# Attention and gated FFN on one core: both heads' probabilities turned together in two 64-row tiles, values before keys

## What is computed

```python
def xattn(q, kv, Wq, Wk, Wv, Wo, bo, mask):    # 16 heads of 64
    qh, kh, vh = split_heads(q @ Wq), split_heads(kv @ Wk), split_heads(kv @ Wv)
    dots = einsum('bhid,bhjd->bhij', qh, kh) * 64 ** -0.5
    dots = where(mask or above the diagonal, -max, dots)
    attn = softmax(dots)
    return einsum('bhij,bhjd->bhid', attn, vh) -> (b, n, 1024) @ Wo + bo

x = x + tanh(g_xattn) * xattn(layernorm(x), ctx, ...)
x = x + tanh(g_ffn) * ffn(layernorm(x), ...)   # three products, absolute maxima over all of x between them
```

## Time and profile before

| what | value |
|---|---|
| median of 3 runs | 1734.68 us (1733.4 to 1737.57) |
| the profiled execution's own time | 1733.58 us |
| its span, first to last instruction | 1731.8 us |
| PE / DVE / ACT / POOL busy | 96% / 77% / 67% / 28% of the span |
| mean granted TensorE clock | 0.982 |
| attention, some | 1150 us of it |

### The profile page before, as it was taken

The page is one execution under the profiler, slowest core; times in us unless marked ns, Lnnn a source line. Parts: engine busy times, 40 slices in busy tenths (PEclk is TensorE's granted clock), DMA queues, the critical chain, the costliest instruction groups (busy, mean ns, idle before and its releaser), DMA issues. The chain is left out here.

```text
span 1731.8 us, 40384 instructions
## 1 busy us (share of the span) xinstructions
PE 1657.9 (96%) x14196; PEld 1407.6 (81%) x14196; DVE 1334.1 (77%) x2273; ACT 1162.8 (67%) x3061; POOL 493.5 (28%) x367
## 2 busy tenths in 40 slices
PE   8999999999999999999999999989997998986998
PEld 6788888888888888888888888878885876875998
DVE  7867768677777786776867778867887999898785
ACT  5656666666566665666666656657676999895665
POOL 2332323223223233232332322310002765560000
PEclk9999999999999999999999999989998999997999
DMA  4110001001100011010100110026775885664664
GB/s 142 67 40 27 28 22 50 24 26 36 30 34 24 26 36 38 26 36 14 50 24 26 36 38 13 14 86 239 283 276 188 298 289 209 230 248 168 212 212 144
DMA packets 60002, 173.55 MB, mean 100 GB/s; under 512 B 4528, under 2 KB 34352, under 8 KB 57008
## 3 DMA queue, kind: packets, MB, share of 16 engines
q1 hardware_dynamic: 59952, 172.90, 28.9%
HBM read 96.86 MB, written 76.02 MB: 100 GB/s over the span
## 5 line engine op out<-in xcount | busy, mean ns | idle before, releaser
L386 POOL TENSOR_TENSOR prob<-prob,rsums 128x512 f32<-128x512 f32 x254 | 266.7, 1050 | 783.5 <-DVE rsums L582 640.7
L428 ACT ACTIVATE prob<-masked,neg_max 128x128 f32<-128x128 f32 x1024 | 396.4, 391 | 77.5 <-DVE neg_max L560 76.5
L428 ACT ACTIVATION_READ_ACCUMULATOR prob<-masked,neg_max 128x1 f32 x1024 | 194.3, 190 | 0.0
L560 DVE TENSOR_REDUCE neg_max<-masked 128x4 f32<-128x512 f32 x254 | 174.3, 686 | 8.8
L558 DVE TENSOR_TENSOR masked<-score,mask_add 128x512 f32<-128x512 f32 x254 | 172.8, 680 | 0.8
L578 DVE COPY probT<-trans 128x512 f32<-128x512 f32 x126 | 86.9, 690 | 108.7 <-PE trans L792 105.8
L792 PE MATMUL trans<-ident,prob 128*128 128x128 f32 x1024 | 160.3, 279 | 0.9 <-POOL prob L406 0.8
L443 ACT ACTIVATE qT<-proj 128x512 f32<-128x512 f32 x128 | 76.7, 599 | 110.8 <-PE proj L757 110.8
L840 PE MATMUL y<-wo_hi,o_hi 128*128 128x256 f32 x508 | 145.5, 286 | 2.1 <-DVE wo_lo L508 2.0
L813 PEld LDWEIGHTS pv<-probT,v_sb 128*64 128x64 f32 x2048 | 109.7, 136 | 46.4 <-issue 44.3
L813 PE MATMUL pv<-probT,v_sb 128*64 128x128 f32 x2048 | 140.1, 279 | 6.5 <-issue 5.8
(11 more groups left out here) (251 smaller groups left out, 4588.1 us busy)
## 6 DMA issues: line engine op xcount, KB each, us to landing
gate<-gate_d SPq DMA_DIRECT2D x30, 768.0 KB, 4.5
n_x<-n_x_d SPq DMA_DIRECT2D x25, 512.0 KB, 5.0
gate_d<-stage SPq DMA_DIRECT2D x8, 1536.0 KB, 6.1
n_u_d<-w_raw SPq DMA_DIRECT2D x16, 768.0 KB, 4.0
stage<-n_u_d SPq DMA_DIRECT2D x16, 768.0 KB, 6.3
gate_d<-gate SPq DMA_DIRECT2D x7, 1536.0 KB, 6.1
x_in<-in_x SPq DMA_DIRECT2D x16, 512.0 KB, 3.9
ctx_in<-in_ctx SPq DMA_DIRECT2D x16, 512.0 KB, 3.6
```

The source lines that it names most:

```text
L386: gp.tensor_tensor(pr, pr, rsums[:, h, :].rearrange("p (b o) -> p b o", o=1).broadcast_to([P, NB, P]), ALU.mult).then_inc(normed, 1)
L428: nc.scalar.activation(prob[:, c % 2, h, b, :], masked[:, h, b, :], ACT.Exp, bias=neg_max[:, h, b:b + 1], accum_out=psums[:, h, b:b + 1]). ...
L560: nc.vector.tensor_reduce(neg_max[:, h, :], masked[:, h], X, ALU.max, negate=True).then_inc(max_done, 1)
```

## The change

Both heads' probabilities of a unit are turned together at the step's start, in 16 transposes instead of 8. Each takes 64 of the 128 queries (one half of the array's rows) and writes 64 columns: queries 0 to 63 to the bank `trans`, queries 64 to 127 to a bank of `proj`, for which `jobs` has a new job "turn" (36 jobs in a group instead of 28; `turn_bank` and `turn_job` give its bank and count). ACT copies both banks to `probT` (`copy_turned`), each copy half of every head's columns; DVE's copy goes. In PE's list the values stand before the keys, and one value job moves from step 0 to step 6. Step 6's output product stands where it does in the other steps. In step 7 t2 and t3 follow the keys directly. ACT takes both heads' exponentials before it copies `kT`; DVE takes the second reciprocal before its other work. `times_v` waits for the two copies, and in steps 0 and 4 also for that step's value copy. At attention's end the FFN's weights go through three banks instead of four.

```diff
     YC = 3
+    V_JOBS = [(0,), (1, 2), (3,), (4,), (5,), (6,), (7,), ()]
     jobs = []
     for c in range(NC):
-        jobs += [(c, "q", 0)]
+        jobs += [(c, "turn", 0), (c, "q", 0)]
         if c == NC - 1:
             jobs += [(c, "t", n) for n in range(KC)]
-        jobs += [(c, "k", 0)]
-        if c < 2:
-            jobs += [(c, "v", 2 * c), (c, "v", 2 * c + 1)]
-        elif c < 6:
-            jobs += [(c, "v", NB + c - 2)]
+        jobs += [(c, "v", n) for n in V_JOBS[c]] + [(c, "k", 0)]
     jobs += [(NC - 1, "t", n) for n in range(KC, 2 * KC)]
...
-                wait(act, transposed, 2 * (u - 2) + h + 1)
+                wait(act, transposed, u - 1)
...
+            def copy_turned(u, b, before):
+                act.wait_ge(transposed, u + 1)
+                wait(act, pv_done, u)
+                nc.scalar.activation(probT[:, :, :, 0:HALF], halves(hand.banks[0]), ACT.Copy).then_inc(first_copied, 1)
+                act.wait_ge(projected[b], before + 1)
+                nc.scalar.activation(probT[:, :, :, HALF:P], halves(proj[b]), ACT.Copy).then_inc(copied[b], 1)
             def step(g, c):
                 u, new, soft, old, more = parts(g, c)
                 if old:
-                    act.wait_ge(transposed, 2 * (u - 2) + 1)
-                    wait(act, pv_done, u - 2)
-                    nc.scalar.activation(probT[:, 0], trans[:], ACT.Copy).then_inc(probT_copied[0], 1)
+                    copy_turned(u - 2, *turn_bank(g, c, u))
...
                     exps(u - 1, c + 1, 0)
+                    exps(u - 1, c + 1, 1)
                 if new:
                     (i, _), = jobs_of(c, "k")
                     b, before = nth(g, i)
...
                 if nxt:
                     high(g, *ts[KC])
-                if soft:
-                    exps(u - 1, c + 1, 1)
-                if nxt:
                     high(g, *ts[KC + 1])
...
-                if old:
-                    dve.wait_ge(transposed, 2 * (u - 2) + 2)
-                    wait(dve, pv_done, u - 2)
-                    nc.vector.tensor_copy(probT[:, 1], trans[:]).then_inc(probT_copied[1], 1)
...
-            def transpose_prob(u, c, h):
-                pe.wait_ge(normed, 2 * u + h + 1)
-                wait(pe, probT_copied[1 - h], u + h)
-                for b in range(NB):
-                    last = nc.tensor.transpose(trans[:, b, :], prob[:, c % 2, h, b, :], ident[:])
-                last.then_inc(transposed, 1)
+            def transpose_prob(u, c, b, before):
+                pe.wait_ge(normed, 2 * u + 2)
+                wait(pe, first_copied, u)
+                wait(pe, copied[b], before)
+                pe.nop(nofuse=True)
+                to = [halves(a) for a in (hand.banks[0], proj[b])]
+                for e in range(NB):
+                    for h in range(2):
+                        for r in range(2):
+                            rows = slice(r * HALF, (r + 1) * HALF)
+                            last = nc.tensor.transpose(to[r][:, h, e, :], prob[rows, c % 2, h, e, :], ident[rows, rows])
+                            if e == NB - 1 and h == 1:
+                                last.then_inc(projected[b] if r else transposed, 1)
...
-            def times_v(u, c, then=None):
-                for h in range(2):
-                    pe.wait_ge(probT_copied[h], u + 1)
+            def times_v(u, c, b, before, then=None):
+                pe.wait_ge(first_copied, u + 1)
+                counts = {b: before + 1}
+                if c % 4 == 0 and then is not None:
+                    for i, n in jobs_of(then[1], "v"):
+                        bank, earlier = nth(then[0], i)
+                        counts[bank] = earlier + 1
+                for bank, n in counts.items():
+                    pe.wait_ge(copied[bank], n)
...
                 if old:
-                    transpose_prob(u - 2, co, 0)
+                    transpose_prob(u - 2, co, *turn_bank(g, c, u))
                 if new:
                     weights_left(g, c, jobs_of(c, "q")[0][0], 0)
...
-                if oldest and c != NC - 2:
+                if oldest:
...
-                if first or second:
-                    pe.wait_ge(w_ready, 2 if first else 5)
-                if new:
-                    weights_left(g, c, jobs_of(c, "k")[0][0], 1)
-                if old:
-                    transpose_prob(u - 2, co, 1)
-                if nxt:
-                    transpose_in(g, *ts[2])
-                if oldest and c == NC - 2:
-                    out_product(u - 3, (c - 3) % NC)
-                if first or third:
-                    pe.wait_ge(w_ready, 3 if first else 6)
+                if first:
+                    pe.wait_ge(w_ready, 3)
                 if new:
                     for i, n in jobs_of(c, "v"):
                         value(g, i, n)
+                if second:
+                    pe.wait_ge(w_ready, 5)
+                if new:
+                    weights_left(g, c, jobs_of(c, "k")[0][0], 1)
                 if nxt:
+                    transpose_in(g, *ts[2])
                     transpose_in(g, *ts[3])
                 if old:
-                    times_v(u - 2, co, (g, c, u) if new else None)
+                    times_v(u - 2, co, *turn_bank(g, c, u), (g, c, u) if new else None)
                 if new:
```

More of the change, by code:

```diff
@@ L111, in jobs_of, with turn_job @@
         return [(i, n) for i, (cc, k, n) in enumerate(jobs) if cc == c and k == kind]
+    no_turn = [jobs.index((c, "turn", 0)) for c in range(2)]
+    no_input = [i for i, (_, kind, _) in enumerate(jobs) if kind == "t"]
     def nth(g, i):
-        skipped = KC // 2 if isinstance(g, int) and g == G - 1 and i == last_k else 0
-        return i % 2, (FIRST + i) // 2 + (NJ // 2) * g - skipped
+        left_out = [a for a in no_turn if not isinstance(g, int) or g > 0 or g == 0 and a < i]
+        if isinstance(g, int) and g >= G - 1:
+            left_out += [a for a in no_input if g == G or a < i]
+        return i % 2, (FIRST + i) // 2 + (NJ // 2) * g - sum(a % 2 == i % 2 for a in left_out)
+    def turn_job(u):
+        if not isinstance(u, int):
+            return None
+        if u >= U:
+            b, before = nth(G, 0)
+            return b, before + u - U
+        return nth(u // NC, jobs_of(u % NC, "turn")[0][0])
     with ExitStack() as st:
@@ L200, in attention @@
         transposed = sem("transposed")
-        probT_copied = [sem(f"probT_copied{h}") for h in range(2)]
+        first_copied = sem("first_copied")
         pv_done = sem("pv_done")
@@ L251, in ffn_weights @@
             kind, k, h = ffn_jobs[n]
-            bank = ffn_banks[n % 4]
+            bank = ffn_banks[n % 3]
             if kind == "gate":
@@ L276, in w_part, with turn_bank @@
             return a[n][:].rearrange("p (k n) -> p k n", k=KC if n < 3 else 1)[:, :, lo:hi]
+        def turn_bank(g, c, u):
+            return turn_job(u) if isinstance(u, int) else nth(g, jobs_of(c, "turn")[0][0])
         def staged(i):
@@ L495, in _ @@
             nc.scalar.activation(o_hi[:], pv[:], ACT.Copy).then_inc(out_high, 1)
-            first_probT(U - 1)
-            for n in range(4):
+            copy_turned(U - 1, *turn_job(U + 1))
+            for n in range(3):
                 ffn_high_part(n)
@@ L500, in _ @@
             nc.scalar.activation(last_hi, hand.banks[1][:], ACT.Copy).then_inc(out_high, 1)
-            for n in range(4, len(ffn_jobs)):
+            for n in range(3, len(ffn_jobs)):
                 ffn_high_part(n)
@@ L588, in step @@
                         nc.vector.tensor_copy(v_sb[:, n % NB, cols], proj[b][:]).then_inc(copied[b], 1)
+                if soft:
+                    dve.wait_ge(exp_done, NB * (2 * (u - 1) + 2))
+                    wait(dve, normed, 2 * (u - 1))
+                    nc.vector.reciprocal(rsums[:, 1, :], psums[:, 1, :]).then_inc(recip_done, 1)
                 if nxt:
@@ L596, in step @@
                     residual(g)
-                if soft:
-                    dve.wait_ge(exp_done, NB * (2 * (u - 1) + 2))
-                    wait(dve, normed, 2 * (u - 1))
-                    nc.vector.reciprocal(rsums[:, 1, :], psums[:, 1, :]).then_inc(recip_done, 1)
                 if nxt:
@@ L726, in _ @@
             nc.vector.tensor_tensor(o_lo[:], hand.banks[1][:], o_hi[:].bitcast(F32), ALU.subtract).then_inc(out_split, 1)
-            ffn_low_part(0)
-            second_probT(U - 1)
-            for n in range(1, 4):
+            for n in range(3):
                 ffn_low_part(n)
@@ L850, in step @@
                 second = isinstance(g, int) and g == 0 and c == 1
-                third = isinstance(g, int) and g == 0 and c == 2
                 oldest = not isinstance(g, int) or 3 <= u < U + 3
@@ L933, in _ @@
                 last.then_inc(hand.x_transposed, 1)
-            for n in range(4, len(ffn_jobs)):
+            for n in range(3, len(ffn_jobs)):
                 ffn_transpose(n)
             for n in range(7 * NB):
```

(2 more changed lines are left out.)

40 lines of the change are left out of this document (15 added, 25 removed).

## The result

The changed kernel takes 1818.06 us (median of 4 runs, 1816.47 to 1821.34), the kernel before 1734.48 beside it: a ratio of 1.0481 [1.0461, 1.0502], 4.8% slower. The forecast was 1767 with a range up to 1803: the direction was right, the loss more than twice what was forecast (83 us for 33).

What follows compares the result with a forecast made beforehand. TensorE was taken to bound the kernel, busy for 1657.9 of 1731.8 us. Groups 1 to 14 add +27 us, the first about +2, the last about +4: +33 on 1734.68, said as 1767 us; range 1748 to 1803.

Steps and rivals of the forecast that it cites:

- Turning: Paired 64-row transposes at each step's start, with tile change and bare load: 0.71 us against 0.94, saving 0.23 per step.
- Rival 1: The two 64-row tiles take turns, so turning takes 0.94 and a step loses 0.21: 1816 us; chance 0.12.
- The late quarter: In six ordinary steps pv's last quarter waits for the key copy and streams 0.09 us late, bounds 0 and 0.2.
- The net of an ordinary step: Turning's saving and the late quarter in an ordinary step: -0.23 + 0.09 = -0.14 us.
- Step 4: Key copy behind eight late exponentials delays pv's last quarter: step of 9.62 us against 8.56, +1.06.
- Step 7: Fourth input transpose waits for the key copy until 8.79 us, then 2.50 to the next step: 11.29 against 9.55, +1.74.
- Added waits: Waits for normalised probabilities at a step's start covered by at least 0.5 us; step 4's value copy wait costs nothing.
- The first group: Group 0: no second statistics, but weight work on VectorE makes ScalarE wait 4.8 us for maxima; about +2 us.
- The last group's +4: No inputs to turn, but maxima waits push exponentials, five steps by 0.7 to 1.1 less 0.14; about +4 us.
- The sum: Middle group +1.95 us, groups 1 to 14 +27, with first and last group together +33 us.
- The Trainium skill's rule of the load by columns: A weight load takes columns / 1.2 ns whatever its rows; a transpose pair would last 0.11 us, turning saving nothing.

Runs made afterwards that it cites:

- Experiment 4: Changed kernel with each head turned in four full-array transposes and copied whole, instead of 64-row tiles copied in halves: 1845.86 us, 1.0656 of the kernel before.
- Experiment 2: Changed kernel with TensorE's wait for the key copy put last, behind the waits for masked scores: 1795.27 us, 1.0363 of the kernel before.
- Experiment 3: Changed kernel with twenty discarded identity transposes between step 7's third and fourth input transposes: 1802.96 us, 1.0406 of the kernel before.
- 1: Changed kernel with the key copy between the two heads' exponentials in step 7 alone: 1785.72 us, 1.0308 of the kernel before.
- 6: Changed kernel with keys in front of the values again in steps 0, 1, 3, 4 and 5: 1824.11 us, 1.0512 of the kernel before.
- 8: Kernel 7 with both layernorms' statistics in front of `o_lo` and step 7's maximum behind the first reciprocal: 1785.33 us, 1.029 of the kernel before.
- 7: Changed kernel with keys first as in 6, key wait last, and step 7's key copy between the heads' exponentials: 1775.97 us, 1.0243 of the kernel before.
- 9: Kernel 7 with step 1 as v1, k, v2, second reciprocal before value copies following keys, step 3's statistics between maxima and first reciprocal: 1733.95 us, 0.998.

## Why the prediction was right and wrong

- **Turning: right.** 0.71 us forecast; the query product starts at 0.64 and its first matmul, with its bare load of 0.11, streams at 0.75. The saving is 0.41 + 0.44 - 0.64 = 0.21, forecast 0.23. Experiment 4 has it as 0.20 to 0.24. Rival 1 (tiles take turns) is refuted by the pairs at 636.90, though its 1816 us is the time that came: a matching sum of a wrong cause.
- **The late quarter: this step failed.** "The waiting quarter then loads at 0.845 and streams at 0.90: 0.09 late", bounds 0 and 0.2. It is 0.38 late, in six steps of every group. I took a restart of 0.045 us from a step 7 row where nothing stands between the wait and the matmul; here register work and another wait stand between. Experiment 2 takes two thirds of the excess away by the order of the waits alone. The order printed ahead shows these instructions, and the prediction named them, but its upper bound didn't price them. The net of an ordinary step is +0.14 to +0.17 instead of -0.14: 6 x 0.29 = 1.7 us a group, 23 us in 13 groups.
- **Step 4: right.** 9.52, forecast 9.62; the masked scores start at 2.86 instead of 3.27, so VectorE's chain did move a little, and the slower restart gave most of that back. (The quarter streamed at 7.4 before, not at the 7.05 that the prediction says, which is step 7's number; its sum does not use it.)
- **Step 7: half.** The stall is right (8.85, forecast 8.79). **"From it to the next step 2.50: 11.29" failed**: 3.99, since the clock fell behind a wait of 1.9 us that had one of 0.3 us shortly before it. No rival had it; the cost of the clock was put at nothing. Where the clock stayed high step 7 takes 11.6, 0.3 more than forecast (PE stands 0.2 us ahead of the next turn); where it fell, 1.2 to 1.5 more than that, in ten of 13 groups. Experiment 3 gives 0.75% for all of the clock.
- **Added waits: right in the middle groups, with a mistake.** PE waits for no normalised probabilities there. Behind the last unit it does, 2.3 us where it was 0.8, which the prediction left out. And the wait of `times_v` for the step's own value copy stands in steps 2 and 6 (its `c` is that of the unit, two steps older), not in 0 and 4, as the texts ahead say.
- **The first group: failed too.** "About +2" was forecast; group 1 starts 11 us later. In group 0 PE waits 2.2 us for a value copy in step 1, where it waited 0.5 for the keys' copy, and 4.0 us for the key copy in step 5, where `pv` stood 2.8, and the granted clock is 0.95 on the mean from 22 to 94 us, for 1.00 before. What each of these costs was not tested. The last group's +4 came out at +1.3.
- **The sum.** The 13 middle groups were forecast to lose 25 us and lost 63.5. The quarter gives 23 of the difference and step 7 gives 17 (1.32 a group on the mean, 1.0 of it clock), less 1 for step 4: 64. So there the account closes. Outside them 8 us were forecast and 20 came, 9 of the excess in group 0, and that part stays open.

## What to carry to other kernels

Moving a step behind its consumer's last input makes the restart part of the path: count every instruction between the last wait and the matmul, and put the wait that comes last at the end of the list. A stall of a matmul engine is not over when its input comes; read the granted clock behind it, and if it fell, cheap work in the gap pays. Before reordering an engine that isn't the bound, list for each of its results who waits and when: three of these kernels (1, 6 and 8) exchanged one late hand-over for another, and the order by need, on VectorE and in step 1, was worth 42 us (experiments 7 and 9).

## What was not expected of the hardware

- The restart behind a semaphore: 0.34 us from the end of the copy to the matmul with another wait and register work behind the wait; with the wait last, scores start 0.19 us earlier.
- TensorE's granted clock falls to its 1.2 GHz level behind waits of 0.3 and 1.9 us in ten of 13 equal groups (75.3 us, and 74.0 where it doesn't), and 20 transposes of the identity, 2.35 us, keep it at 1.00. The Trainium skill, "TensorE: Matmul & The Clock Gate", section "Part 4: PE-mode transpose", says that transposes don't count as busy for the clock in the same way. Experiment 3's filler is nothing but transposes, and the clock stayed: for holding the full clock, the measurement decides against the page. Whether transposes alone can raise it no run here shows.
- Two 64-row tiles, each with a load of 128 columns and a stream of 64, take (637.38 - 637.01) / 6 = 0.062 us a pair, both loads included. The Trainium skill's rule of the load by columns, quoted in the prediction, would make it 0.11; the measurement decides against it for this form.
